# Value weights of a cross attention split in two ways: the second quad's in whole pieces beside the first quad's values, the rest in half pieces one quad ahead

## What is computed

```python
q = (inputs_q @ Wq).reshape(b, sq, H, HD) * (1.0 / np.sqrt(HD))
k = (inputs_kv @ Wk).reshape(b, skv, H, HD)
v = (inputs_kv @ Wv).reshape(b, skv, H, HD)
scores = jnp.einsum('bqhd,bkhd->bhqk', q, k)
attn = jax.nn.softmax(scores, axis=-1)
ctx = jnp.einsum('bhqk,bkhd->bqhd', attn, v).reshape(b, sq, H * HD)
return ctx @ Wo
```

## Time and profile before

| | us |
|---|---|
| median of 3 runs | 1664.24 |
| lowest and highest | 1660.63, 1665.55 |
| the profiled execution's own time | 1665.45 |
| its span in the trace | 1663.7 |
| TensorE busy | 1621.7 (97%) |
| VectorE busy | 1076.8 (65%) |
| ScalarE busy | 695.0 (42%) |

### The profile page before, as it was taken

The page is one execution under the profiler, slowest core; times in us unless marked ns, Lnnn a source line. Parts: engine busy times, 40 slices in busy tenths (PEclk is TensorE's granted clock), DMA queues, the critical chain, the costliest instruction groups (busy, mean ns, idle before and its releaser), DMA issues.

```text
span 1663.7 us, 23437 instructions
## 1 busy us (share of the span) xinstructions
PE 1621.7 (97%) x9220; PEld 1279.7 (77%) x9220; DVE 1076.8 (65%) x1708; ACT 695.0 (42%) x940; POOL 131.2 (8%) x218
## 2 busy tenths in 40 slices
PE   8998999999999999999999999999989999999998
PEld 7876888888888888888888888888747756554454
DVE  4555777777777677777777779999473751643333
ACT  3443444444444444444444446666231321322221
POOL 0000000000100000010000001111000000021110
PEclk9999999999999999999999999999989999999999
DMA  6987445554644545555454554335211516579994
GB/s 218 280 273 220 129 127 133 140 133 121 190 119 129 139 126 135 127 173 139 127 133 124 137 133 121 100 91 161 105 77 52 201 52 249 223 219 418 424 423 185
DMA packets 122189, 282.99 MB, mean 170 GB/s; under 512 B 7456, under 2 KB 77280, under 8 KB 115936
## 3 DMA queue, kind: packets, MB, share of 16 engines
q1 hardware_dynamic: 99776, 200.74, 38.3%
q0 software_dynamic: 22304, 80.75, 16.3%
HBM read 206.99 MB, written 74.48 MB: 169 GB/s over the span
## 4 chain that ended last, share of the span: by engine, by line
PE 68%; issue 17%; DVE 5%; DMA 5%; ACT 3%; POOL 2%; SPq 0%; DVEq 0%; POOLq 0%; ACTq 0%
PE bank L41 15%; PE bank L436 15%; PE bank L405 13%; PE bank L451 7%; PE bank L2041 5%; PE bank L1660 3%; PE bank L2080 2%; DMA wk_raw<-in_wv 2%; PE bank L2066 2%; DMA v_dram<-v_out 1%; PE bank L2070 1%; POOL v_back L982 1%; PE bank L478 1%; PE bank L2026 1%; DMA wv_parts<-wv_dram 1%
## 5 line engine op out<-in xcount | busy, mean ns | idle before, releaser
L436 PE MATMUL bank<-wv_parts,cT_hi 128*128 128x512 f32 x1024 | 335.6, 392 | 6.6 <-DMA wv_parts<-wv_dram 3.9
L436 PEld LDWEIGHTS bank<-wv_parts,cT_hi 128*128 128x128 f32 x1024 | 193.6, 189 | 47.9 <-issue 4.3
L806 DVE TENSOR_TENSOR e_lo<-S,e_hi 128x1024 fp32r<-128x1024 f32 (+1 forms) x129 | 156.8, 1215 | 92.7 <-ACT e_hi L605 89.7
L405 PE MATMUL bank<-cT_hi,wk_hi 128*128 128x512 f32 x512 | 205.0, 400 | 1.4 <-DVE cT_lo L738 1.4
L405 PE MATMUL bank<-cT_hi,wk_lo 128*128 128x512 f32 x512 | 200.6, 392 | 0.0
L436 PE MATMUL bank<-wv_parts,cT_lo 128*128 128x512 f32 x512 | 200.4, 391 | 0.0
L596 ACT ACTIVATE S<-S 128x1024 f32<-128x1024 f32 (+1 forms) x129 | 135.9, 1053 | 152.6 <-DVE S L785 152.1
L405 PE MATMUL bank<-cT_lo,wk_hi 128*128 128x512 f32 x512 | 199.2, 389 | 0.0
L605 ACT CAST e_hi<-S 128x1024 fp32r<-128x1024 f32 (+1 forms) x129 | 134.9, 1046 | 142.3 <-PE bank L451 137.4
L798 DVE TENSOR_TENSOR esum<-esum,S 128x512 f32<-128x512 f32 x210 | 145.0, 690 | 71.7 <-ACT S L596 68.1
L451 PE MATMUL bank<-e_hi,v_back 128*128 128x256 f32 x880 | 167.7, 288 | 0.7 <-DMA v_back<-v_dram 0.7
(11 more groups left out here) (285 smaller groups left out, 2606.1 us busy)
## 6 DMA issues: line engine op xcount, KB each, us to landing
w<-in_w_moe SPq DMA_DIRECT2D x32, 2304.0 KB, 15.1
v_dram<-v_out SPq DMA_DIRECT2D x112, 512.0 KB, 5.0
v_back<-v_dram POOLq DMA_DIRECT2D x110, 512.0 KB
ctx_nat<-in_ctx SPq DMA_DIRECT2D x8, 1024.0 KB, 4.8
ctx_raw<-in_ctxT SPq DMA_DIRECT2D x7, 1024.0 KB, 8.4
v_dram<-v_back SPq DMA_DIRECT2D x14, 512.0 KB, 4.9
v_late<-v_dram POOLq DMA_DIRECT2D x14, 512.0 KB
wv_dram<-wv_piece SPq DMA_DIRECT2D x12, 512.0 KB, 5.3
```

What stands on the lines that cost most here:

```text
L405: t = e.matmul(banks[b][:], l, r, start=(c == 0 and m == 0), stop=(c == DT - 1 and m == 2))
L436: t = e.matmul(banks[b][:], l, r, start=(c == 0 and m == 0), stop=(c == DT - 1 and m == 2))
L806: e.tensor_tensor(lo, S[:, of_chunk(j, m), :], hi.bitcast(F32), ALU.subtract).then_inc(e_split, 1)
```

## The change

Only quad 1's value weights are still prepared in whole pieces in the first pass: four pieces, at chunks 3 and 4. The key weights of head 1 are loaded one chunk earlier.

The weights of quads 2 and 3 are prepared in 8 half pieces each (256 of 512 columns), in the heads of the quad before last: quad 2's in heads 0 to 2, quad 3's in heads 4 to 6, at chunks 2, 4 and 6 of the first two of these heads and chunks 2 and 4 of the third. A half piece uses `wk_raw` alone: it lands in its second half (128 KB), ACT rounds it into the first half, DVE writes the low part over the second half, SP spills both (256 KB). So `wk_raw` is taken in heads 0, 1, 2, 4, 5, 6 until then, and in these heads `load_wk(h + 2)` moves from chunk 0 to the end of chunk 6, where it waits for the last half piece's spill to land (`half_in`).

`load_wv` counts its two transfers on two semaphores, `v_in[2]` and `v_in[3]`, and the first unit's first six matmuls wait for the first transfer only.

```diff
         def piece_at(j, m):
-            i = 2 * (j - 1) + m
-            return i if 0 <= i < WV_PIECES else None
+            i = 2 * (j - 3) + m
+            return i if 0 <= i < DT else None
+        HALF = QW // 2
+        HALF_STEPS = [(0, 2), (0, 4), (0, 6), (1, 2), (1, 4), (1, 6), (2, 2), (2, 4)]
+        def half_at(h, j):
+            g, step = h // HPQ, (h % HPQ, j)
+            return g * 2 * DT + HALF_STEPS.index(step) if g < QUADS - 2 and step in HALF_STEPS else None
+        def half_place(i):
+            g, k = divmod(i, 2 * DT)
+            return g + 2, k // 2, slice(k % 2 * HALF, (k % 2 + 1) * HALF)
+        def halves_done(i):
+            return 1 + DT + i
...
             def load_wk(h):
-                    if h == 1:
-                        e.wait_ge(wv_split, WV_PIECES + 1)
-                    if h == 2:
-                        e.wait_ge(*v_spilled(KVT - 1))
+                    if h == 1:
+                        e.wait_ge(wv_split, DT + 1)
+                    if h >= 2 and (h - 2) // HPQ < QUADS - 2:
+                        e.wait_ge(half_in, 16 * halves_done(len(HALF_STEPS) * ((h - 2) // HPQ) + len([s for s in HALF_STEPS if s[0] <= (h - 2) % HPQ])))
                     e.dma_start(wk_raw[:], a["wk"][h]).then_inc(wk_in, 16)
+            def load_half(h, i):
+                g, c, ws = half_place(i)
+                e.wait_ge(wk_split, h + 2)
+                if i == 0:
+                    e.wait_ge(*v_spilled(KVT - 1))
+                e.wait_ge(half_in, 16 * halves_done(i))
+                e.dma_start(wv_raw[:, HALF:], a["wv"][g, :, c, ws]).then_inc(wv_in, 16)
+            def spill_half(i):
+                g, c, ws = half_place(i)
+                e.wait_ge(wv_split, halves_done(i + 1))
+                e.dma_start(wv_dram[g - 1, c // 2, :, :, c % 2, ws], wv_raw.rearrange("p (l w) -> p l w", l=2)).then_inc(half_in, 16)
...
-                if j == NCH - 2:
+                if j == NCH - 3:
                     load_wk(1)
...
-                        load_wk(h + 2)
+                        if half_at(h, 2) is None:
+                            load_wk(h + 2)
...
                     for u in units(h, j):
                         spill(u)
+                    if half_at(h, j) is not None:
+                        spill_half(half_at(h, j))
+                    if half_at(h, j + 1) is not None:
+                        load_half(h, half_at(h, j + 1))
+                    if j == NCH - 2 and half_at(h, 2) is not None:
+                        load_wk(h + 2)
...
-                    if kt == 0 and c == 0:
-                        if g == 0:
-                            e.wait_ge(wv_split, 1)
-                        else:
-                            e.wait_ge(v_in[2], 32 * g)
+                    if kt == 0 and g == 0 and c == 0:
+                        e.wait_ge(wv_split, 1)
+                    elif kt == 0 and g and c % 2 == 0:
+                        e.wait_ge(v_in[2 + c // 2], 16 * g)
...
+            def round_half(i):
+                e.wait_ge(wv_in, 16 * halves_done(i + 1))
+                e.copy(wv_raw[:, 0:HALF].bitcast(F32R), wv_raw[:, HALF:]).then_inc(wv_rounded, 1)
...
+            def split_half(i):
+                e.wait_ge(wv_rounded, halves_done(i + 1))
+                e.tensor_tensor(wv_raw[:, HALF:].bitcast(F32R), wv_raw[:, HALF:], wv_raw[:, 0:HALF], ALU.subtract).then_inc(wv_split, 1)
...
                 for m in range(2):
-                    e.dma_start(wv_parts[:, :, 2 * m:2 * m + 2, :], wv_dram[g - 1, m].bitcast(F32R)).then_inc(v_in[2], 16)
+                    e.dma_start(wv_parts[:, :, 2 * m:2 * m + 2, :], wv_dram[g - 1, m].bitcast(F32R)).then_inc(v_in[2 + m], 16)
```

More of the change, by code:

```diff
@@ L185, in build @@
         wv_dram = nc.dram_tensor("wv_dram", [QUADS - 1, 2, P, 2, DT // 2, QW], F32, kind="Internal").ap()
-        WV_PIECES = (QUADS - 1) * DT
+        HALF = QW // 2
+        HALF_STEPS = [(0, 2), (0, 4), (0, 6), (1, 2), (1, 4), (1, 6), (2, 2), (2, 4)]
         v_last, = place(WORK + 4 * KVT * T, ("v_last", [P, HPQ, 2, XHD], F32))
@@ L269, in v_ring @@
             turns = late // 2 if n < TAIL else (TAIL - LATE * NCH) // 2 * (b < 2) + (n - TAIL) // 4
-            return (v_back, v_late, v_tail0, v_tail1)[b], v_in[b], 16 * (turns + 1 + (LATE * NCH if b == 0 else 2 * (QUADS - 1) if b == 2 else 0))
+            return (v_back, v_late, v_tail0, v_tail1)[b], v_in[b], 16 * (turns + 1 + (LATE * NCH if b == 0 else QUADS - 1 if b >= 2 else 0))
         def piece_at(j, m):
-            i = 2 * (j - 1) + m
-            return i if 0 <= i < WV_PIECES else None
+            i = 2 * (j - 3) + m
[8 more added lines that the diff above has]
+            return 1 + DT + i
         def starts_quad(h):
@@ L316, in load_piece @@
                     e.wait_ge(wv_split, i + 1)
-                e.dma_start(wv_raw, a["wv"][g + 1, :, c, :]).then_inc(wv_in, 16)
+                e.dma_start(wv_raw, a["wv"][1, :, i, :]).then_inc(wv_in, 16)
             def spill_piece(i):
-                g, c = divmod(i, DT)
                 e.wait_ge(wv_split, i + 2)
-                e.dma_start(wv_dram[g, c // 2, :, :, c % 2, :], wv_piece[:].bitcast(F32)).then_inc(half_in, 16)
+                e.dma_start(wv_dram[0, i // 2, :, :, i % 2, :], wv_piece[:].bitcast(F32)).then_inc(half_in, 16)
+            def load_half(h, i):
[9 more added lines that the diff above has]
+                e.dma_start(wv_dram[g - 1, c // 2, :, :, c % 2, ws], wv_raw.rearrange("p (l w) -> p l w", l=2)).then_inc(half_in, 16)
             def spill(u):
@@ L680, in scalar_cross @@
                         round_v(u)
+                    if half_at(h, j) is not None:
+                        round_half(half_at(h, j))
             for h in range(LATE, XH - 1):
@@ L763, in keep_max @@
                     else:
-                        e.wait_ge(half_in, 16 * (WV_PIECES + 1))
+                        e.wait_ge(half_in, 16 * (DT + 1))
                     e.tensor_reduce(mxr[:], mx[:].rearrange("p a t -> p t a"), AX.X, ALU.max).then_inc(max_folded, 1)
@@ L909, in vector_cross @@
                             split_v(u)
+                    if half_at(h, j) is not None:
+                        split_half(half_at(h, j))
             for h in range(LATE, XH - 1):
@@ L986, in load_wv @@
                 e.wait_ge(v_projected, KVT * g)
-                e.wait_ge(half_in, 16 * (DT * g + 1))
+                e.wait_ge(half_in, 16 * halves_done(2 * DT * (g - 1)))
                 for m in range(2):
-                    e.dma_start(wv_parts[:, :, 2 * m:2 * m + 2, :], wv_dram[g - 1, m].bitcast(F32R)).then_inc(v_in[2], 16)
+                    e.dma_start(wv_parts[:, :, 2 * m:2 * m + 2, :], wv_dram[g - 1, m].bitcast(F32R)).then_inc(v_in[2 + m], 16)
             def largest_score(h):
@@ L1460, in build @@
             ("hT", [P, DT, T], F32), ("xn3", [P, TT, D], F32), ("g3", [P, 64], F32))
-        landed = {"w_up": (wk_in, 16 * XH + 16), "w_down": (wv_in, 16 * (WV_PIECES + 2)), "w_exp": (wqo_in, 16 * len(qo_order) + 16),
+        landed = {"w_up": (wk_in, 16 * XH + 16), "w_down": (wv_in, 16 * (halves_done(2 * DT * (QUADS - 2)) + 1)), "w_exp": (wqo_in, 16 * len(qo_order) + 16),
                   "w_gate": (x_in, 32), "w_q4": (att_w_in[0], 32), "w_o4": (att_w_in[1], 32), "scalars": (att_w_in[2], 32),
@@ L1898, in build @@
         slots_out, slots_in, y_out, rows_turned = sems("slots_out slots_in y_out rows_turned")
-        ROWS_OUT = 16 * (WV_PIECES + 1 + TT)
+        ROWS_OUT = 16 * (halves_done(2 * DT * (QUADS - 2)) + TT)
         VALUES_IN = [max(value for _, sem, value in map(v_ring, range(NH)) if sem is v_in[n]) for n in range(N_ROWS)]
```

1 line of the change is left out of this document (removed).

## The result

The changed kernel takes 1674.1 us (median of 4 runs, 1673.75 to 1674.71) against 1664.68 before. The ratio is 1.0055, with a 95% interval of 1.0042 to 1.0067: it is slower by 9 us, and outside the range of 1656 to 1672. The profiled execution took 1674.71 us.

The account below looks back on a forecast made before the run. TensorE, busy for 97% of the span, was taken as the bound, so only its waits and clock count. From the profiled 1665.45 us, -3.8 - 4.1 + 7.2 = -0.7 gave 1664.8, 1663.5 on the median's scale; range 1656 to 1672.

Parts of the forecast that it names:

- The first pass: Before the heads: removing 8 of 12 pieces cuts TensorE's idle, 3.8 us gained, with 1.8 and 4.4 as ends.
- the two certain idles: First pass, at 68 and 139 us: both idles go, 0.6 + 1.2 = 1.8 us.
- The four idles: First pass: TensorE's notable idles, worth 4.4 us; two at chunks 3 to 5 hold 2.65, of which 2.0 gained.
- The count per half: Quad 1's weights: six matmuls run inside the wait (1.36 us), the clock holds (2.7); 4.1 us gained, ends 0 and 4.1.
- The wait of near 3 us: Quad 1's first unit: cut in two around a wait near 3 us, with PEclk at 1.00 after it.
- The half pieces themselves: In the heads: 16 added loads, roundings, subtractions and spills fit into idle time, costed at nothing.
- The key weights: Heads 0, 1, 4, 5, chunk 6: the load waits for the half piece's spill, 1.8 us four times, 7.2 us.
- L1 + L2 - 6.1: TensorE's wait for the key weights in head 1's times: 1.8 us with L1 + L2 taken as 7.9.
- L1: Chunk 6: landing time of the half piece's spill, taken as 4.8 us, ends 3.3 and 5.3.
- L2: After that spill: landing time of the key weights' load, taken as 3.1 us, upper end 5.0.
- The slower rival: Heads: key weights come very late, L1 + L2 is 10.3, waits of 4.2 us each, 1673 us; chance 0.15.
- 3.2 us a wait: Key weights: from this wait (L1 + L2 above 9.3) the slower rival decides, cost passing the gains by 5.

Follow-up runs that it names:

- experiment 2: Changed kernel with both transfers of a quad's value weights counted on one semaphore again: 1677.5 us, ratio 1.0068.
- experiment 1: Changed kernel with half pieces at chunks 2 and 4 of all four heads, key weights' load at the end of chunk 5: 1656.3 us, ratio 0.9944.
- experiment 11: As experiment 1, with each half piece also ahead of its chunk's value unit: 1655.2 us, ratio 0.9943.
- experiment 7: Changed kernel without half pieces, quads 2 and 3 computed with quad 1's weights, key weights loaded at chunk 0: 1654.3 us, ratio 0.9941.
- experiment 5: Changed kernel with each half piece rounded, split and spilled ahead of its chunk's value unit: 1660.8 us over 10 runs, ratio 0.9972.
- experiment 3: Changed kernel with 12 small matmuls in front of the four key products that wait: 1669.2 us, ratio 1.0018.
- experiment 4: Changed kernel with 6 small matmuls in front of the four key products that wait: 1665.4 us, ratio 1.0009.
- experiment 10: As experiment 1, but with the key weights' load at the end of chunk 6 instead of chunk 5: 1656.9 us, ratio 0.9954.
- experiment 6: Kernel before with the count per half alone: 1661.5 us, ratio 0.9981.
- experiment 8: Kernel before, no half pieces; in heads 0, 1, 4, 5 the key weights' load stands at chunk 6's end, waiting for its value spill: 1668.6 us, ratio 1.0026.

## Why the prediction was wrong

**The first pass** was right in kind: the two certain idles are gone, and behind the pieces about 1.6 us are left of 2.65, hidden parts included. That 3.9 us came where 3.8 were forecast is partly luck. The four idles account for 2.9 of the 3.9 us; the rest lay in delays too small to be listed as idle, as in the chunk from 46.8 us, which took 15.3 us before and 15.1 now. And over all traces the gain is 4.8 us, more than the 4.4 that the forecast gave as its upper end.

**The count per half** was right in kind and a little low: 5.2 us at that place where 4.1 were forecast. The count is worth 3.3 of them (experiment 2); the rest is an earlier landing (0.9), which I hadn't put in, and a clock that cost less in the one trace than in the other (1.0). The wait of near 3 us that was foretold for the second half was 1.6, for the same reason.

**The half pieces themselves** were rightly costed at nothing: with the 16 of them the last head's output comes within a microsecond of the run without them (experiments 1 and 11 against 7).

**The key weights** were the step that failed, in two terms. The formula held: "the wait is L1 + L2 - 6.1", and 6.3 + 2.7 - 6.1 = 2.9 us is what the trace shows. But L1 was put at 4.8, the value spill's own time at that place, as if being half as large made up for going behind it. It is queued behind that spill and landed 2.2 us after it: 6.3 us, and 3.1 with the order turned round (experiment 5). The range's end of 5.3 for L1 was too low too: it was the median of the first pass' spills, whose place in the queue I hadn't asked for.

The second term wasn't in the sum at all: the clock. I had priced its fall at quad 1's weights, by the rows, and did not ask the same of the waits that I was adding. With 1.8 us of wait the question seemed idle; at 2.9 it is 1.72 us more each time, 6.9 in all, as experiments 3 and 4 show. The two terms together are 18.6 us instead of 7.2, so 11.4 too few; the gains were 1.2 more than forecast. That is nearly the whole miss: -3.9 - 5.2 + 18.6 = +9.5, where -0.7 was forecast and the medians differ by 9.4.

The slower rival named the right mechanism, and its forecast of 1673 us came close, in part by luck: it had 4.2 us a wait, all of it idle, where it was 2.9 of idle and 1.7 of clock. With the clock counted, its 3.2 us a wait are reached with an idle of 1.5, if the clock falls there, and are passed with the 2.5 us of the shortest idle of the four. It would have deserved more than 0.15. An estimate by the fit of the Trainium skill ("DMA: Bandwidth & Descriptors", "Anatomy of one DMA"), 2.6 us for 256 KB, comes near the load that runs alone (2.7) and the spill at the head of the queue (3.1), and is less than half of the spill behind another (6.3). The page gives it per transfer on the GpSimd path and doesn't say for what load; in these traces it is a price for an empty queue. The rule of the Trainium skill, "Trainium Kernel Development and Optimization", Key Constraints, that transfers of different issuers share the engines, isn't what decides here: GpSimd's read of `v_back` is issued within 0.4 us of the half piece's spill both times, at 6.3 us and at 3.1, and what changed is the order on SP's own queue.

**Still open:** why the load took 1 us longer at one place of experiment 3, what makes experiment 10's heads the longest of the three, and at which idles the clock falls in executions that weren't traced.

## What to carry to other kernels

A prefetch moved behind other work is priced by when it lands in its queue, with what stands ahead of it and what the other queues run at that moment; the size of a transfer says little, and here it landed behind the transfer ahead of it, 2.2 us later though it was half as large. Every idle that is added to a busy TensorE should be asked twice: for its length, and for what the work behind it costs if the clock falls. A wait that can't be removed is cheaper broken in two, by whatever part of the work is already there. And where two traces are to be compared, the stages that nothing touched should be taken out first.

## What the runs showed of the hardware

- The clock fell at idles of 2.52 to 2.89 us at all four places of the changed kernel, at 2.45 to 2.87 us at the same places of experiment 2, and at 3.52 to 3.96 us at quad 1's weights. It held through the idles of 1.6 us and less that experiments 4, 5 and 6 left at these places, in the one execution of each that was traced.
- A short idle is no guarantee. Where head 14 is finished, the clock fell behind an idle of 1.34 us in two of the 13 traces (experiments 3 and 8) and held behind the same idle in the others. In the untouched rest it stood at 0.50 for 3.4 to 17.1 us, and the rest took 485.3 to 492.8 us.
- In the changed kernel it fell only after TensorE had resumed: at 1.00 while idle (213 to 214 us), at 0.59 in 216 to 217. The cost lies in the work behind the wait and is not seen in the list of waits; TensorE's busy time shows it.
- The same spill of 256 KB took 6.3 us behind a spill of 512 KB and 3.1 ahead of it. At the other three places it was 6.0 to 6.7 behind and 2.5 to 2.7 ahead.
